# A quantised feed-forward block, from a loop of two passes to two written-out halves woven into its neighbours

## The chip, the cores and the metric

The kernel runs on one core of one Trainium2 chip. The metric is the device time of one execution in microseconds, lower is better. A core has five engines with queues of their own, which meet only through semaphores: TensorE (PE; its weight loads are PEld), VectorE (DVE), ScalarE (ACT), GpSimd (POOL) and SyncE (SP), which here issues the DMAs.

## The reference, cut to what matters

A four-layer network with 4 x 256 tokens of 256 features and a context of 4 x 256 x 64. Each layer adds a gated attention and a gated feed-forward to `x`. The change touches the end of layer 1 and all of layer 2:

```python
# layer 1, feed-forward (causal attention inside; h, mod as the code names them)
gate_pre = h @ W_in_base.T + mod * (h @ A) @ B
mlp_out  = silu(gate_pre) * (h @ W_up_base.T) @ W_down.T
x = x + tanh(g_ffn[1]) * (residual + mlp_out)
# layer 2, attention: a sigmoid of two dot products with the context, mixed with the normed rows
xij = sigmoid(si[:, :, None] + sj[:, None, :] + b)
x = x + tanh(g_xattn[2]) * (0.6 * xij + 0.4 * layernorm(x))
# layer 2, feed-forward: 256 -> 1024 -> 256, both with quantised rows and ternary weights
def bitlinear158(x, w, b): return act_quant(rms_norm(x)) @ weight_quant(w).T + b
h = gelu(silu(bitlinear158(layernorm(x), w1, b1)))
x = x + tanh(g_ffn[2]) * bitlinear158(layer_norm(h, ln_g, ln_b), w2, b2)
# act_quant: scale = 127 / max|x| of the row; round(x * scale) clipped to [-128, 127]
```

Layer 3 is an attention (`l3x`, stream C below) and a soft mixture of experts.

## The kernel before

The 1024 tokens lie in `xs`, eight tiles of 128 rows by 256 columns; a half is four tiles (two batches, `T0 = 4`). The stages run one after the other: layer 0 with its experts (to about 430 us), weights turned, stream A of `attention` (the cross attention `l1x` and the causal attention `l1f` of layer 1), the feed-forward of layer 1 with the norms of the slot vectors of layer 3 woven in, a loop of two passes over the quantised layer 2, stream C (`l3x`) and the soft experts.

**Attention.** A stream is cut into groups of eight heads, and each engine walks slices `sl` with steps `k` from 0 to 7. In slice sl TensorE computes the scores by key of group sl (`by_key`), the scores by query of group sl + 2 (`by_query`, from which VectorE takes maxima), and turns the queries and keys of group sl + 3. The slices start at sl = -3, so three slices are a prologue without an exp. Stream C has eight groups, two for each batch. For the causal attention a mask is added by a multiply with the identity: L966 writes 512 columns of a bank for the second query tile (32 times in all, for k from 2 to 5 of eight groups), L1007 512 columns for the first key tile (32 times). Both masks are zero in half of these columns. ACT's `norm` makes the normed rows of a batch once `ln_x` says that the statistics are there; for stream C `all_stats` takes them over all eight tiles.

**Feed-forward of layer 1.** `gate_and_up(h, f)` for 2 halves x 8 slices of 128 hidden columns (TensorE), a silu (L1573, ScalarE), a product (L2067 in `hidden`, VectorE); then four `down(h, i)` a half (L1210) and the additions in `add_down` (L2073). In between stand `slot_products` (L1220), `turn_slot_parts`, `spread_slots` (L1235) and, on VectorE, `slot_norms` and `scale_slots` (L2091). A gate may start once the product two before it has freed its banks.

**The quantised block.** All engines meet at a barrier (`end_of_batch`: each arrives, GpSimd clears the stage's semaphores, L445, and lets all go on), ahead of the loop and behind each of its passes. A pass takes one half: the context is copied and turned (L1262), `sj` (L1265), sigmoids (L1587); on VectorE `si`, statistics (L1667 to L1671, a root in 11 small steps), the sums L2125 to L2129, statistics again, L2135, and `quantise`; turned rows (L1273), up products (L1282), VectorE's L2158, silu (L1594), gelu (L1597), statistics of the hidden rows (L2168), gain and bias (L1678, L2175), squares (L1601), `quantise` again with the maximum L2139 and the passes L2150, L2152 and L2153; turned hidden rows (L1290 and the copy q2T), down products (L1295), and the addition L2188. TensorE fills two waits with `keep_clock`: 50 and 40 multiplies of L589 that nobody reads. GpSimd does nothing in the loop. SyncE issues the late loads for layer 3 once the feed-forward's downs are done, then arrives at the first barrier.

The order on each engine is written by hand, and each queue is strictly in that order. Eight PSUM banks are given out by hand too: gates use 0 to 3, downs 4 and 5, the slot norms 6 and 7.

Of the kernel before, what the change touches and what calls it, by code (L numbers as in the profile page):

```python
# [88 lines left out]
def maxima_landed(stream, s):  # L89
# [14 lines left out]
     "slot_sums_ps", "slot_sums", "gathered_ps", "gathered", "soft_out"),  # L104
    ("cT_ps", "sj_ps", "si", "l2x_sig", "l2x_done", "l2f_q1", "q1T_ps", "q1T", "l2f_pre", "l2f_up", "l2f_silu",
     "l2f_gelu", "l2f_stats", "l2f_ln", "l2f_sq", "l2f_q2", "q2T_ps", "q2T", "l2f_down"))
# [22 lines left out]
def flamingo(nc, I, out):  # L129
    with ExitStack() as ctx:  # L130
        sems, batch_sems = {}, []

        def once(name):

            if name not in sems:
                sems[name] = ctx.enter_context(nc.semaphore(name))
            return sems[name]
# [74 lines left out]
        quad = sb("quad", [P, 4, 32])  # L212
        region = top[0]
# [80 lines left out]
        after_operands = top[0]  # L294
        kTx = sb("kTx", [P, 2, 8, N], BF16)
# [22 lines left out]
        hT = sb("hT", [P, DC, TOKENS])  # L318
        at_f = sb("at_f", [P, B, NT, D])
        keep = top[0] - 2 * 8192  # L320


        top[0] = after_late
        gu = sb("gu", [P, HALVES, F1 // P, 512])
        sgf = [sb(f"sgf{k}", [P, 512]) for k in range(2)]
        mu2 = sb("mu2", [P, DC, SLOTS])
        atT = sb("atT", [P, DC, TOKENS])
        modT = sb("modT", [R, TOKENS])
        mh = sb("mh", [R, TOKENS])
        assert top[0] <= keep  # L330


        top[0] = after_late
        h2 = sb("h2", [P, T0, F1])
        q2 = sb("q2", [P, T0, F1], BF16)
        q2T = sb("q2T", [P, F1 // P, T0 * P], BF16)
        q1 = sb("q1", [P, T0, D], BF16)
        q1T = sb("q1T", [P, DC, T0 * P], BF16)
        xn2 = sb("xn2", [P, T0, D])
        tmp2 = sb("tmp2", [P, T0, D])  # L340
        bn2 = sb("bn2", [P, T0, 2, 6])
        c2 = sb("c2", [P, T0, CD])
        cT2 = sb("cT2", [CD, T0 * P])
# [18 lines left out]
        rcc = sb("rcc", [P, 16])  # L362

# [45 lines left out]
        assert high[0] <= nc.sbuf_usable_end  # L409

# [43 lines left out]
        def _(sp):  # L454
# [92 lines left out]
            for n in rowsF:  # L547
                W(rowsF[n][:, :], I[n].partition_broadcast(P)).then_inc(once("late_rows"), 16)
            sp.wait_ge(S("ffn_down"), T0 * HALVES)
# [7 lines left out]
            end_of_batch(sp)  # L557
            sp.wait_ge(once("batch_cleared"), B // 2 + 1 + B // 2)
# [19 lines left out]
        def _(pe):  # L578
# [304 lines left out]
            def attention(stream):  # L883
# [56 lines left out]
                def by_query(s, k):  # L940
# [16 lines left out]
                    if L == "l1f":  # L957
# [7 lines left out]
                        else:  # L965
                            mm(to[:, :], identb[:, :], mask_q[:, 1:2, :].broadcast_to([P, 2, N]), start=True, stop=False,  # L966
                               skip_group_check=True)
# [25 lines left out]
                def by_key(s, k):  # L993
# [3 lines left out]
                    to = bank[3 + n % 2]  # L997
                    if k == 0:
# [5 lines left out]
                    if L == "l1f":  # L1004
                        ti = 0 if k < 4 else 1
                        if ti == 0:
                            mm(to[:, :], identb[:, :], mask_t[:, 0:1, :].broadcast_to([P, 2, N]), start=True, stop=False,  # L1007
                               skip_group_check=True)
# [103 lines left out]
                for sl in range(-3, S_ + (1 if stream == "A" else 2)):  # L1112
                    for k in range(8):
# [58 lines left out]
            pe.wait_ge(S("at_done"), 2 * B)  # L1172
            for h in range(HALVES):
# [8 lines left out]
            for h in range(HALVES):  # L1182
# [3 lines left out]
                last.then_inc(S("mod_ps"), 1)  # L1186

# [49 lines left out]

            for f in range(F1 // P):
                gate_and_up(0, f)
            for f in range(F1 // P):  # L1240
# [3 lines left out]
                if f == 1:  # L1244
                    slot_products()
# [1239 lines left out]
```

## Time and profile before

| | us |
|---|---|
| three timed runs, median (lowest to highest) | 1382.35 (1380.15 to 1384.04) |
| the profiled execution, its own time | 1384.49 |
| its span in the trace | 1382.7 |
| PE, PEld, DVE, ACT, POOL busy | 1111.1, 689.8, 756.2, 513.8, 323.4 |
| chain that ended last: PE, DVE, ACT, issue | 69%, 20%, 4%, 4% |

Read the busy shares by stretch, not over the whole: the chain that ended last is TensorE's for two thirds, but there is a stretch of 160 us in which it is VectorE's. In a row of the timeline stand the start, the duration, engine, line, operation, what is written from what is read, the count, and in brackets how long the engine was idle before it and what released it. Rows of TensorE overlap: the pitch between starts counts, not the duration.

### The profile page before, as it was taken

What the parts mean: (1) busy time and instruction counts of PE and PEld (TensorE: products, weight loads), DVE (VectorE), ACT (ScalarE), POOL (GpSimd) and SP (SyncE); (2) the same over time, 40 slices, a digit from 0 to 9 for tenths busy, and PEclk for the clock granted to TensorE, in tenths of its full rate; (3) what the DMA queues carried; (4) which work ended last, traced back from release to release, by engine and by line L of the source; (5) the groups of instructions that cost most, each with busy time, mean ns of one, the idle gap of its engine ahead of it and who ended that gap; (6) DMA issues with size and microseconds to landing.
All of it is one profiled execution on the core that took longest, in us unless ns stands there. A gap on an engine that the chain in (4) does not pass through costs nothing.

```text
span 1382.7 us, 19444 instructions
## 1 busy us (share of the span) xinstructions
PE 1111.1 (80%) x6805; PEld 689.8 (50%) x6805; DVE 756.2 (55%) x1716; ACT 513.8 (37%) x857; POOL 323.4 (23%) x624
## 2 busy tenths in 40 slices
PE   3247999999997687887989999952535887899997
PEld 2125888888886432333555436621313443465565
DVE  4553445445444567766465111258777766577544
ACT  1112333333333565644445310014232554445443
POOL 4004344333434455324233200000001520000000
PEclk9557999999999668987999998976777899999999
DMA  6000111111301200000000200010000000000000
GB/s 152 0 0 24 46 46 46 46 46 46 106 23 59 71 2 3 2 2 2 3 2 3 107 0 0 0 46 1 0 0 0 3 2 2 0 1 9 8 1 16
DMA packets 62440, 32.05 MB, mean 23 GB/s; under 512 B 47104, under 2 KB 61072, under 8 KB 62112
## 3 DMA queue, kind: packets, MB, share of 16 engines
q1 hardware_dynamic: 62368, 31.10, 8.5%
q8 instruction: 44, 0.72, 0.2%
q14 instruction: 28, 0.23, 0.1%
HBM read 29.64 MB, written 1.05 MB: 22 GB/s over the span
## 4 chain that ended last, share of the span: by engine, by line
PE 69%; DVE 20%; ACT 4%; issue 4%; POOL 1%; SPq 1%; DMA 0%; POOLq 0%; DVEq 0%; ACTq 0%
PE bank L655 15%; PE bank L671 7%; PE bank L763 4%; PE bank L1045 3%; DVE mx L1945 3%; PE bank L1195 2%; PE bank L979 2%; PE bank L878 2%; PE bank L846 2%; PE bank L1210 2%; PE bank L1197 2%; PE bank L808 2%; PE bank L589 2%; PE bank L1025 2%; PE bank L1078 2%
## 5 line engine op out<-in xcount | busy, mean ns | idle before, releaser
L1945 DVE TENSOR_REDUCE mx<-bank 128x2 f32<-128x512 f32 (+1 forms) x176 | 118.1, 689 | 94.3 <-PE bank L979 45.2
L1503 ACT ACTIVATE prob<-bank 128x512 f32<-128x512 f32 x176 | 102.7, 597 | 105.4 <-PE bank L1025 78.8
L1342 ACT ACTIVATE hhi<-hh 128x512 fp32r<-128x512 f32 x72 | 45.5, 632 | 153.1 <-DVE hh L1782 140.5
L1778 DVE TENSOR_TENSOR hu<-bank,sg 128x512 f32<-128x512 f32 x64 | 44.2, 691 | 101.4 <-PE bank L655 101.4
L589 PE MATMUL bank<-mask_q,identb 128*128 128x512 bf16 x180 | 48.5, 439 | 62.5 <-DVE h L2175 49.1
L655 PE MATMUL bank<-xh,wh 128*128 128x512 f32 x288 | 91.5, 399 | 0.7 <-POOL wl L2293 0.7
L655 PE MATMUL bank<-xh,wl 128*128 128x512 f32 x288 | 90.6, 395 | 0.0
L655 PE MATMUL bank<-xlo,wh 128*128 128x512 f32 x288 | 90.2, 394 | 0.0
L1770 DVE TENSOR_TENSOR hlo<-hh,hhi 128x512 fp32r<-128x512 f32 x72 | 57.2, 794 | 50.8 <-ACT hhi L1342 50.8
L2293 POOL TENSOR_TENSOR wl<-wraw,wh 128x512 fp32r<-128x512 f32 x72 | 80.5, 1118 | 13.0 <-POOL wh L2290 13.0
L1381 ACT ACTIVATE sg<-bank 128x512 f32<-128x512 f32 x72 | 43.0, 598 | 65.0 <-PE bank L655 64.9
L589 PEld LDWEIGHTS bank<-mask_q,identb 128*128 128x128 bf16 x180 | 19.5, 110 | 93.7 <-DVE h L2175 50.1
L655 PEld LDWEIGHTS bank<-xh,wh 128*128 128x128 f32 x288 | 54.4, 189 | 14.5 <-POOL wl L2293 1.6
L655 PEld LDWEIGHTS bank<-xlo,wh 128*128 128x128 f32 x288 | 54.4, 189 | 13.4
L655 PEld LDWEIGHTS bank<-xh,wl 128*128 128x128 f32 x288 | 54.4, 189 | 12.4
L763 PE MATMUL bank<-mun,xT 128*128 128x512 f32 x128 | 58.1, 597 | 1.2 <-ACT xw L1342 1.2
L671 PE MATMUL bank<-hhi,wh 128*128 128x512 f32 x144 | 56.8, 394 | 0.9 <-DVE hlo L1770 0.9
L671 PE MATMUL bank<-hhi,wl 128*128 128x512 f32 x144 | 56.9, 395 | 0.0
L671 PE MATMUL bank<-hlo,wh 128*128 128x512 f32 x144 | 56.1, 390 | 0.0
L979 PE MATMUL bank<-kTx,qT 48*128 48x256 bf16 x256 | 52.5, 314 | 3.7 <-DVE kTx L1909 3.1
L1025 PE MATMUL bank<-qT,kTx 51*128 51x512 bf16 x128 | 52.9, 429 | 2.2 <-ACT prob L1503 2.1
L1945 DVE TENSOR_REDUCE mxc<-bank 128x2 f32<-128x512 f32 x64 | 42.6, 686 | 17.0 <-PE bank L979 16.0
(445 smaller groups left out, 2367.2 us busy)
## 6 DMA issues: line engine op xcount, KB each, us to landing
wraw<-in_L_ffn_wg_dram SPq DMA_DIRECT2D x64, 64.0 KB, 2.3
wraw<-in_L_ffn_wu_dram SPq DMA_DIRECT2D x64, 64.0 KB, 2.4
wraw<-in_L_ffn_wd_dram SPq DMA_DIRECT2D x32, 128.0 KB, 2.5
l_raw<-in_L_ffn_w_dram SPq DMA_DIRECT2D x2, 1024.0 KB, 7.0
mun<-in_L_ffn_mu_dram SPq DMA_DIRECT2D x1, 2048.0 KB, 7.9
xs<-in_x_dram SPq DMA_DIRECT2D x1, 1024.0 KB, 5.8
w1s<-in_L_ffn_W_dram SPq DMA_DIRECT2D x2, 512.0 KB, 7.9
stage<-in_L_ffn_W_in_base_dram SPq DMA_DIRECT2D x1, 1024.0 KB, 8.1
```

The lines of the kernel that those rows point to most:

```text
L589: mm(bank[k][:, :], identb[:, :], mask_q[:, :, :], start=True, stop=True, skip_group_check=True)
L655: last = mm(bank[4 + (n + m) % 4][:, :], w[k % 2][:, m, cc * P:(cc + 1) * P], v[:, cc, tok], start=j == 0 and cc == 0, stop=j == 2 and cc ...
L671: last = mm(bank[2 * m + h][:, :], w[k % 2][:, 2, m * P:(m + 1) * P], v[h][:, :], start=False, stop=last_pair and j == 2, skip_group_check ...
L763: last = mm(bank[n % 2][:, :], xT3[b % 2][:, cc, i * P:(i + 1) * P], mun[:, cc, ch * 512:(ch + 1) * 512], start=cc == 0, stop=cc == 1)
L979: last = mm(to[:, f * N:(f + 1) * N], t.qT[rows, s % 4, u, i * P:(i + 1) * P], key_operand(L, b, s, 8 * g + 2 * j + f, rows, slice(0, N)), ...
L1025: last = mm(to[:, :], key_operand(L, b, s, 8 * g + 2 * j, rows, slice(ti * P, (ti + 1) * P)), t.qT[rows, s % 4, u:u + 2, :], start=True, s ...
L1342: return act.activation(dst, src, ACT.Copy, scale=scale)
L1503: act.activation(t.prob[k][:, :], bank[3 + n % 2][:, :], ACT.Exp).then_inc(S("probs"), 1)
L1770: tt(hlo[k % 2][:, :], hh[k % 2][:, :], hhi[k % 2][:, :].bitcast(F32), ALU.subtract)\
L1778: tt(hu[k % 2][:, :], bank[4 + (n + 1) % 4][:, :], sg[k % 2][:, :], ALU.mult).then_inc(once("up_used"), 1)
L1945: V.reduce_max(out_, bank[n % 3][:, :].rearrange("p (h t) -> p h t", h=heads), AX, negate=True)\
L2293: G.tensor_tensor(low[:, cols, :], wraw[k][:, cols, :], high[:, cols, :].bitcast(F32), ALU.subtract)\
```

## The change

- **Masks.** L966 and L1007 write only the 256 columns of the diagonal blocks; the other half of the bank is written by the product that follows, since the first multiply opened the bank.
- **Barrier.** The loop `with Fori(0, B // 2)` and its two barriers go, and the one ahead of it moves to the end of stream A, ahead of the feed-forward. Stage semaphores count through to the end.
- **Layer 2's sigmoids** for both halves are made ahead of the gates: contexts are turned into banks 6 and 7, copied, multiplied with `l2wj` into banks 4 and 5, and ScalarE writes `sig[0]` and `sig[1]`.
- **The block in two halves.** Half 0 is written between the gates of the second half of the feed-forward; its end, with the first steps of half 1, follows the last downs. The rest of half 1 is written into stream C's prologue: turned inputs, up products and silu at (sl, k) = (-3, 7), gelu at (-2, 6), everything from the statistics of the hidden rows to the last addition at (-1, 7). Statistics for stream C are taken for each half by itself, and the `norm` of batches 2 and 3 waits for the second.
- **Feed-forward.** The slot work moves into half 0; the four downs of half 0 follow the first gate of half 1 in a row; those of half 1 use banks 0 and 1 and wait for all products.
- **Engines.** Norm, centring, rounding's second step and the scaling of the hidden rows become ScalarE activations with a bias from `l2v`; the gain and the `b2` row become GpSimd products; VectorE keeps statistics, sums, maxima and the first step of rounding. The clip is gone (the rounded value can't leave the range).
- **keep_clock** goes from the block.

```diff
@@ TensorE, by_query and by_key of the causal attention
-    mm(to[:, :], identb[:, :], mask_q[:, 1:2, :].broadcast_to([P, 2, N]), start=True, ...)
+    mm(to[:, :].rearrange("p (f n) -> p f n", f=2)[:, :, P:N], identb[:, :],
+       mask_q[:, 1:2, P:N].broadcast_to([P, 2, P]), start=True, ...)
-    mm(to[:, :], identb[:, :], mask_t[:, 0:1, :].broadcast_to([P, 2, N]), start=True, ...)
+    mm(to[:, :].rearrange("p (f n) -> p f n", f=2)[:, :, 0:P], identb[:, :],
+       mask_t[:, 0:1, 0:P].broadcast_to([P, 2, P]), start=True, ...)
@@ TensorE, by_key
+    if stream == "C" and n == 0:
+        pe.wait_ge(S("l2_rows"), 2 * T0)
@@ TensorE, stream C's slices
+    if (sl, k) == (-3, 7):
+        turn_inputs(1)
+        for i in range(T0):
+            l2_up(1, i)
+    if (sl, k) == (-1, 7):
+        l2_last(1)
@@ TensorE, ahead of and in the feed-forward
     attention("A")
     pe.wait_ge(S("at_done"), 2 * B)
+    end_of_batch(pe)
+    pe.wait_ge(once("batch_cleared"), B // 2 + 1)
...
+    for h in range(HALVES):
+        pe.wait_ge(S("modT"), h + 1)
+        for i in range(T0):
+            last = pe.transpose(bank[6 + h][0:CD, i * P:(i + 1) * P], ctxs[:, T0 * h + i, :], ident[:, :])
+        last.then_inc(S("c_turned"), 1)
+    for h in range(HALVES):
+        pe.wait_ge(S("cT2"), h + 1)
+        pe.wait_ge(S("mh"), h + 1)
+        mm(bank[4 + h][:, :], l2wj[:, :], cT8[:, h * 512:(h + 1) * 512], ...).then_inc(S("sj_ps"), 1)
...
+    # down: n == 0 waits for l2_sig, n == T0 for all 16 ffn_gu; banks (4, 0)[h] + n % 2
+    # L2_BANKS = ((4, 5, 6), (3, 4, 5)); use n of a half has bank n % 3 of these, and waits for the reader of n - 3
+def l2_last(h):
+    turn_hidden(h, 0); turn_hidden(h, 1); l2_down(h, 0); turn_hidden(h, 2)
+    l2_down(h, 1); turn_hidden(h, 3); l2_down(h, 2); l2_down(h, 3)
+for f in range(F1 // P):
+    gate_and_up(0, f)      # f == 1: slot_products, 3: turn_slot_parts, 5: spread 0 and 1, 6 and 7: spread 2, 3
+gate_and_up(1, 0)
+for i in range(T0):
+    down(0, i)
+for f in range(1, F1 // P):
+    gate_and_up(1, f)      # f == 4: turn_inputs(0), 5: l2_up(0, 0), (0, 1), 6: l2_up(0, 2), (0, 3)
 for i in range(T0):
     down(1, i)
...
-with pe.Fori(0, B // 2) as b:
...
-    keep_clock(3, 50)
...
-    keep_clock(0, 40)
...
+l2_last(0)
+pe.wait_ge(S("ffn_out"), 2 * T0)
 attention("C")
@@ ScalarE, behind the gates of half 0
+gate_silu(1, 0); gate_silu(1, 1); l2_normed(0); gate_silu(1, 2); l2_centred(0); gate_silu(1, 3)
+l2_first_quantised(0); gate_silu(1, 4); l2_inputs_turned(0); gate_silu(1, 5); l2_silu(0, 0); l2_silu(0, 1)
+gate_silu(1, 6); l2_silu(0, 2); l2_silu(0, 3); gate_silu(1, 7); l2_gelu(0, i); l2_z(0, i)      # i: all four
+l2_normed(1); l2_square(0, i); l2_second_quantised(0, i); l2_centred(1); l2_hidden_turned(0, i)
@@ ScalarE, stream C: (-3, 7): l2_inputs_turned(1), l2_silu(1, i); (-2, 6): l2_gelu(1, i)
+    if (sl, k) == (-1, 7):
+        # for all i each: l2_z, l2_square, l2_second_quantised, l2_hidden_turned
@@ VectorE, behind the products of half 0
+hidden(1, 0); scale_slots(3); add_down(0, i)                                  # i: all four
+l2_norm(0); hidden(1, 1); l2_mean(0); hidden(1, 2); l2_round_inputs(0); hidden(1, 3); hidden(1, 4)
+l2_pre(0, 0); l2_pre(0, 1); hidden(1, 5); l2_pre(0, 2); l2_pre(0, 3); hidden(1, 6); hidden(1, 7)
+l2_stats(0, 0); l2_stats(0, 1); add_down(1, 0); l2_stats(0, 2); l2_stats(0, 3); add_down(1, 1)
+l2_norm2(0); add_down(1, 2); add_down(1, 3); l2_norm(1); l2_shift(0); l2_round_hidden(0)
+l2_mean(1); l2_add(0); stats_of(step, 0.25, range(T0)); dve.sem_inc(S("ln_x"), 1); l2_round_inputs(1)
@@ VectorE, stream C: (-3, 7): l2_pre(1, i)
+    if (sl, k) == (-1, 7):
+        # l2_stats(1, i), then:
+        l2_norm2(1); l2_shift(1); l2_round_hidden(1); l2_add(1)
+        stats_of(step, 0.25, range(T0, 2 * T0))
+        dve.sem_inc(S("ln_x"), 1)
@@ VectorE, the new steps whose length matters
+def l2_shift(h):
+    for i in tiles:
+        dve.wait_ge(S("l2_zg"), T0 * h + i + 1)
+        tt(h2[:, i, :], h2[:, i, :], rowsF["L2_ffn_ln_b"][:, :], ALU.add).then_inc(S("l2_ln"), 1)
+    dve.wait_ge(S("l2_ln"), T0 * (h + 1))
+    step(V.tensor_reduce(l2v[:, 44:48], h2[:, :, :], AX, ALU.max, apply_absolute_value=True))
@@ GpSimd
+def l2_bias(h):          # rows + b2, four tiles in one product, once l2_xc is there
+def l2_gain(h):
+    for i in range(T0):
+        pool.wait_ge(S("l2_z"), T0 * h + i + 1)
+        G.tensor_tensor(h2[:, i, :], h2[:, i, :], rowsF["L2_ffn_ln_g"][:, :], ALU.mult).then_inc(S("l2_zg"), 1)
+l2_bias(0); l2_gain(0)   # then the clearing of b2s; in stream C l2_bias(1) at sl = -3, l2_gain(1) at sl = -1
@@ ScalarE, stream C's norm: one slice later (k == 0, sl + 4), batch 2 waits for ln_x 2
```

## Rows read from the trace of the kernel before

**Rows 1.** Busy time by stretch: window, length, busy (instructions) of each engine, clock, DMA.

```profile
core 0: us, PE busy (x) PEld busy (x) DVE busy (x) ACT busy (x) POOL busy (x), PEclk, DMA share, GB/s
655.00:772.70 117.70, 104.61 (x1418) 61.38 (x1416) 58.87 (x129) 58.50 (x100) 31.71 (x74) 0.96 0.03 10
...
783.20:901.70 118.50, 116.32 (x370) 63.51 (x369) 23.38 (x48) 11.58 (x19) 1.01 (x3) 0.96 0.00 0
901.70:983.70 82.00, 39.54 (x184) 19.15 (x184) 61.03 (x158) 25.54 (x31) 0.00 (x0) 0.71 0.08 20
983.70:1062.30 78.60, 39.28 (x184) 18.54 (x184) 60.94 (x158) 25.54 (x31) 0.00 (x0) 0.72 0.00 0
```

**Rows 2.** Timeline of the feed-forward, TensorE: gates, slot products, downs.

```profile
787.89 1.98 PE L1195 MATMUL bank<-hT,winT 128*128 128x512 f32 x4
...
792.58 1.98 PE L1195 MATMUL bank<-hT,winT 128*128 128x512 f32 x4
...
833.59 9.93 PE L1220 MATMUL bank<-ones,mu 128*128 128x1 f32 x64
...
850.28 1.98 PE L1195 MATMUL bank<-hT,winT 128*128 128x512 f32 x4
...
894.05 7.17 PE L1210 MATMUL bank<-wdT,gu 128*128 128x256 f32 x32 [1.71 <-DVE xs L2073]
```

**Rows 3.** Timeline at two of the barriers (902 and 984).

```profile
905.81 1.28 ACT L1342 ACT_TABLE_LOAD   x1 [24.40 <-POOLq L445]
...
983.22 0.48 DVE L2188 SCALAR_TENSOR_TENSOR xs<-bank,st,xs 128x256 f32 x1 [0.39 <-PE bank L1295]
985.06 1.28 ACT L1342 ACT_TABLE_LOAD   x1 [5.84 <-POOLq L445]
```

**Rows 4.** Groups by line and shape in the second pass: busy us, mean ns | idle before.

```profile
L2158 DVE SCALAR_TENSOR_TENSOR h<-bank,st,row_L_ffn_b 128x512 f32<-128x512 f32 x8 | 5.6, 746 | 5.2 <-PE bank L1282 4.7 <-DVE h L2158 0.2
L1295 PE MATMUL bank<-w2qT,q2T 128*128 128x256 bf16 x32 | 5.1, 334 | 0.0
L2175 DVE SCALAR_TENSOR_TENSOR h<-h,rs,row_L_ffn_ln_b 128x1024 f32<-128x1024 f32 x4 | 4.9, 1282 | 0.0
...
L2168 DVE BATCH_NORM_STATS2 bn<-h 128x6 f32<-128x512 f32 x8 | 4.8, 676 | 1.8 <-ACT h L1597 1.8
L2139 DVE TENSOR_REDUCE st<-h 128x4 f32<-128x4096 f32 x1 | 4.4, 4420 | 0.0
...
L1597 ACT ACTIVATE h<-h 128x1024 f32<-128x1024 f32 x4 | 3.9, 1045 | 0.0
...
L1667 DVE BATCH_NORM_STATS2 bn<-xs 128x6 f32 x8 | 2.8, 413 | 0.4 <-DVE st L2120 0.3
...
L1654 DVE TENSOR_TENSOR nw<-rs,ve 128x4 f32<-128x4 f32 x12 | 2.0, 163 | 0.4
```

**Rows 5.** Groups by line and shape of GpSimd over the whole span: its two-input products.

```profile
L2444 POOL TENSOR_TENSOR mu<-mun 128x4096 f32<-128x4096 f32 x1 | 7.0, 7013 | 16.7 <-DMA mun<-in_L_ffn_mu_dram 16.7
...
L2330 POOL TENSOR_TENSOR left<-qkf,qst 128x256 f32<-128x256 f32 x8 | 5.4, 670 | 0.6
...
L2412 POOL TENSOR_TENSOR qr<-xnf,row_L_ffn_ln_w 128x512 f32<-128x512 f32 x4 | 5.1, 1268 | 0.7 <-POOL tmp L2412 0.7
```

**Rows 6.** Timeline of stream C's prologue: norm of two batches, first query copy, point P.

```profile
1070.56 2.07 ACT L1479 ACTIVATE xnc<-xs,nmx,rsx 128x256 f32<-128x256 f32 x4 [12.62 <-DVEq L2195]
...
1077.42 0.69 DVE L1909 COPY qTc<-bank 96x1024 bf16<-96x1024 bf16 x1 [0.62 <-PE bank L918]
...
1090.27 2.04 DVE L1945 TENSOR_REDUCE mxc<-bank 128x2 f32<-128x512 f32 x3
```

**Rows 7.** Timeline in the causal attention, TensorE: a mask multiply and what follows.

```profile
742.46 0.39 PE L966 MATMUL bank<-mask_q,identb 128*128 128x512 bf16 x1
...
742.68 0.38 PE L970 MATMUL bank<-kTf,qT 96*128 96x256 bf16 x2
...
742.90 0.38 PE L1007 MATMUL bank<-mask_t,identb 128*128 128x512 bf16 x1
```

**Rows 8.** Instructions of one line: duration ns as min/median/max.

```profile
L1195 PE MATMUL bank<-hT,winT x64: 592/592/1201, 783.2 to 877.4; 128*128 128x512 f32 x64
```

More of the change, by code:

```diff
@@ L133, in once @@
         def once(name):
+            if name in STAGES[2]:
+                return S(name)
             if name not in sems:
@@ L1523, in attention @@
                             norm(groups[sl + 5][1])
-                        if stream == "C" and k == 5 and inside(sl + 5) and groups[sl + 5][1] >= 2 and groups[sl + 5][2] == 0:
-                            norm(groups[sl + 5][1])
+                        if stream == "C" and k == 0 and inside(sl + 4) and groups[sl + 4][1] >= 2 and groups[sl + 4][2] == 0:
+                            if groups[sl + 4][1] == 2:
+                                act.wait_ge(S("ln_x"), 2)
+                            norm(groups[sl + 4][1])
                         if k == 2 and inside(sl - 1):
@@ L2093, in _, with l2_add @@
+            def l2_add(h):
+                dve.wait_ge(S("l2_bias"), h + 1)
+                for i in tiles:
+                    row = l2_rows_of(h, i)
+                    dve.wait_ge(S("l2_down"), T0 * h + i + 1)
+                    stt(out=row, in0=of_l2(h, DOWN_USE[i])[0][:, 0:D], scalar=l2v[:, 48 + i:49 + i], in1=row,
+                        op0=ALU.mult, op1=ALU.add).then_inc(S("l2_rows"), 1)
+                dve.wait_ge(S("l2_rows"), T0 * (h + 1))
             for f in range(F1 // P):
@@ L2193, in _ @@
-            step = Steps(dve, S("dve_step"))
-            all_stats(step, 0.25)
+                if f == 4:
+                    l2_scores(0)
+                    l2_scores(1)
+                if f >= 5:
+                    scale_slots(f - 5)
+            dve.wait_ge(once("late_rows"), len(rowsF) * 16)
+            hidden(1, 0)
+            scale_slots(3)
+            for i in tiles:
+                add_down(0, i)
+            l2_norm(0)
+            hidden(1, 1)
+            l2_mean(0)
+            hidden(1, 2)
@@ new lines, in _ @@
+            l2_round_inputs(0)
+            hidden(1, 3)
+            hidden(1, 4)
+            l2_pre(0, 0)
+            l2_pre(0, 1)
+            hidden(1, 5)
+            l2_pre(0, 2)
+            l2_pre(0, 3)
+            hidden(1, 6)
+            hidden(1, 7)
+            l2_stats(0, 0)
+            l2_stats(0, 1)
+            add_down(1, 0)
+            l2_stats(0, 2)
+            l2_stats(0, 3)
+            add_down(1, 1)
+            l2_norm2(0)
+            add_down(1, 2)
+            add_down(1, 3)
```

546 lines of the change are left out of this document (343 added, 203 removed).

## Prediction

> **What bounds the kernel now.** I read, in this order, busy time by stretch, the timeline of each stretch, the groups by line of the second pass of the quantised loop, and what its ends waited for. The stretches [rows 1] show two regimes. The causal attention (655 to 773) is a TensorE stage, 104.6 of 117.7 us busy; the feed-forward (783 to 902) is one more strongly, 116.3 of 118.5, with VectorE busy for 23.4, ScalarE for 11.6 and GpSimd for 1.0. The two passes of the quantised block (902 to 984 to 1062) are the reverse: VectorE 61 of 79 to 82 us, GpSimd nothing, and TensorE's 39 us are mostly keep-clock multiplies that compute nothing. Each pass is one dependence chain on VectorE with short hops to the others, and they run one after the other. Then comes the prologue of the second attention stream, to 1090, in which the engines wait in turn. So 189 us in which no engine is full stand behind 119 us in which only one is. The change moves work from the first into the second.
>
> **Frame.** Durations are from one execution: span 1382.7 us, timed at 1384.49, which is 2.1 above the median of the three timed runs, 1382.35. I subtract from 1384.5 and then take 2 off. All is measured to one point P, at which VectorE starts the maxima of slice sl = 0 of stream C, 1090.27 [rows 6]; behind it the change alters only the place of two norms.
>
> **Diagonal masks.** 32 mask multiplies of L966 and 32 of L1007 go from 512 to 256 columns. A 512-column one takes a pitch of 0.22 us, and the two 256-column ones behind it share 0.22 [rows 7]. 64 x 0.11 = 7.0 us of TensorE. The stage is 89% TensorE [rows 1]; the rest of it waits for copies and maxima that don't shrink, so 3 to 7 arrive; I take 5.
>
> **The head of the feed-forward.** The barrier now stands ahead of it. Its price is the way from VectorE's last result of a pass (983.70) to ScalarE's start, 985.06, less a hop: 1.3 us [rows 3]. New on TensorE ahead of the first gate: two sets of four f32 context transposes, the first beside the second tanh, then a wait for ScalarE's copy of the second set (0.6 us and two hops of 0.2), then two 512-column f32 products of two passes each. A pass of 512 columns has a pitch of 0.43 to 0.5 (four in 1.98 [rows 2]), so 0.5 for the set, 1.0 for the copy, 1.8 for the products: 3.3 to 3.5. The gates start at 783.2 + 1.3 + 3.5 = 788.0. The eight sigmoids (0.5 each by [rows 6], and a table load of 1.3 [rows 3]) are covered by the first gate.
>
> **Half 0 of the feed-forward.** A gate-and-up takes 4.68 us (787.89 to 792.58), the slot products 9.9, the gate behind them 6.8 because the clock had fallen, two downs 7.2 less 0.4 of overlap [rows 2]. Nine gates 42.1, slot products 10, slow gate 2.2, four downs 13.5, spreading the slots with a wait for their norms 3.2: T = 859.0, the end of the four downs. Merely a new order, no cost.
>
> **Half 0 of the quantised block, beside gates 1 to 7.** Prices [rows 4]: a root 2.2 us (11 steps of 0.2), statistics of four rows 1.4, of four hidden rows 4.8, a 1024-column pass of VectorE over two tensors 1.2, one of a hidden half from PSUM 0.75, ScalarE 0.5 for 256 columns [rows 6] and 1.0 for 1024. Relative to T:
> First norm (statistics 1.4, sum 1.2, aggregate, root, scales) done at 6.6. ScalarE's norm to 8.7. Mean sent at 12.3, but its root holds VectorE to 14.5, so hidden(1, 2) is late and TensorE waits 1.1 us. Inputs rounded at 18.6, quantised 19.2, turned 20.6. Up products wait for their three banks: 1.9 us on TensorE, twice. The last gate ends at 38.5. The downs of half 1 now use banks 0 and 1 and wait for hidden(1, 7), 1.4 us; they end at 53.2. So the feed-forward ends at 912, not 901.7: it pays 10 us.
> Behind it VectorE is the chain again: norm of half 1 to 59.7, shift to 64.6, the 4.4 us maximum to 69.0, root and scales to 72.4, rounding to 75.4, mean of half 1 to 81.1. ScalarE's centring of half 1 stands ahead of the turned hidden copies, so these start at 81; copies, turns and downs alternate over three banks, the last row is added at 88.1, statistics of its four tiles end at 92.5. ln_x comes at 951.5, against 1070.5 now.
>
> **GpSimd's gain.** The gain multiply leaves VectorE for GpSimd. No row has 1024 columns of two f32 inputs there. 256 columns take 0.67, 512 take 1.26, 4096 of one tensor with itself 7.0 [rows 5]. Bounds: 1.75 (a quarter of the last), 2.45 (the slope of the first two). It has two tensors, as those two have, so 2.45; four are 9.8 us. In half 0 they hide behind the last downs and the norm of half 1. In half 1 nothing hides them. While they run, VectorE shifts the rows before, an operation with two SBUF inputs. No row shows such a pair side by side: 0 to 1.2 us for each of three overlaps; I take 3 us in all.
> The Trainium skill (GPSIMD Engine Reference, Key points) says that GpSimd shares its SBUF interfaces with VectorE and contends with VectorE instructions that have two SBUF inputs. By that rule the upper end holds, 1 us above my sum; no row of before shows it.
>
> **The prologue, with the front of half 1 in it.** From the norm (1070.56) to P took 19.7 us [rows 6]. Now, relative to T: norm at 92.6, half 1's inputs rounded on VectorE at 95.9, queries and keys by 101, then in sl = -3 the turned inputs, eight up products and eight VectorE passes of 0.75, to 109.4. The slices sl = -2 and -1 take VectorE 12.3 more, as before (1077.42, less its copy, to 1090.27): 121.7. ScalarE's silu, gelu and two table loads (10.8 us) fit beside.
>
> **The tail of half 1, at (sl, k) = (-1, 7).** It stands in every queue ahead of sl = 0: VectorE's maxima, TensorE's by_key(0, 0) and ScalarE's first exp are behind it. It is serial: statistics 4.9, root 3.2, first z 1.2, gains 9.8 + 3, last shift 1.3, maximum 4.45, root and scales 3.45, first rounding 0.8, four quantised rows 4.0 on ScalarE (all ahead of the first turned copy), the alternation of copies, turns, downs and adds 8.7 (four copies of 1.0 and four downs of 1.3 [rows 4], less their overlap), statistics of four tiles 4.6. Sum 49.4, less 2.8 where rounding and quantising overlap: 46.6. P' = 859.0 + 121.7 + 46.6 = 1027.3. So 63.0 us are gained to P, though some 47 of a pass of 79 stay in the open.
>
> **Removed.** Two barriers of 1.3 and one of 4.1, at 902, which waited for SyncE to issue its late loads [rows 3]: these are inside the 63, as are the keep-clock multiplies. VectorE didn't wait for those (TensorE waited for it), so they give nothing, and without them turns and downs run at the lower clock, counted above. SyncE now issues the late loads beside the block.
>
> **Sum.** 1384.5 - 63 - 5 = 1316.5 on the profiled basis, 1314.5 on the median's: 1315.
>
> **Rivals.**
> (a) The tail is longer. GpSimd slowed to the full (1 to 4 us), 0.2 us at some 30 hand-overs not in my sum (6), gates waiting for VectorE at six more places, 1 us each (6). For it: in a pass of today VectorE is idle for 18 of 79 us [rows 1]. 1325 to 1332. Chance 0.24.
> (b) The tail is shorter: gains at 1.75 without contention (6 us), masks worth all of 7. 1302 to 1308. Chance 0.18.
> (c) The change does what its name promises, all of half 1 beside the prologue: another 40 us, 1275. Against it, all three queues have the tail ahead of sl = 0. Chance 0.02.
> (d) Slower than before, by the clock. If gates stall on VectorE, TensorE's granted clock falls from 2.4 to 1.2 GHz, as for the gate from 843 to 850, where a multiply took 1.20 instead of 0.59 [rows 8]. Seven gates and eight downs at the lower level cost 33 + 27 = 60 us; with (a) on top it is 1385 to 1392. It decides from the point at which nearly every gate stalls; I count waits of 1.1 and 1.4 us in 54, and TensorE is busy for 116.3 of 118.5 today. Chance 0.03.
> (e) The masks give nothing because the maxima's path binds: 1320, inside the forecast.
> The forecast itself, 1308 to 1325: 0.53.
>
> **Range and chances.** 1301 to 1336 leaves out (c), (d) and the outer ends of (a) and (b), together 0.2 at most. 0.3% (4 us) is about what a measurement of this kernel can tell from no change. Faster 0.97, same 0.01, slower 0.02 (the upper part of (d)).
>
> **What will show it.** On the new trace: the first gate near 783 (788 less the masks), four downs in a row that end near 854, the last L1-down near 907; gains of 1.8 to 3.5 us each on GpSimd; VectorE idle ahead of the shifts of half 1 but hardly ahead of those of half 0; the first exp of stream C at 1016 to 1022; TensorE's clock at its upper level through the feed-forward, below it in the tail. The core is wrong if the tail isn't 40 to 55 us long, or if the stretch from the first gate to the last L1-down grew by more than 12 us from 118.5.

## The result, and the profile after

| | us |
|---|---|
| changed kernel, four timed runs, median (lowest to highest) | 1329.76 (1327.55 to 1335.26) |
| kernel before, beside it | 1382.86 (1380.15 to 1384.04) |
| ratio, 95% interval | 0.9625 (0.9592 to 0.9657) |
| profiled execution of the changed kernel, its own time; span | 1327.55; 1325.7 |

The change gains 53 us (57 between the two profiled spans, 1382.7 and 1325.7). 1315 was forecast, with a range of 1301 to 1336: the time lies in the range, 15 above the forecast, where rival (a) was put.

The changed kernel by stretch, to be held against [rows 1]: causal attention, feed-forward from the first gate to the last down, from there to `ln_x`, the prologue of stream C with the front of half 1, the tail of half 1. Columns: window, length, busy (instructions) of each engine, granted clock, DMA.

```profile
core 0: us, PE busy (x) PEld busy (x) DVE busy (x) ACT busy (x) POOL busy (x), PEclk, DMA share, GB/s
650.00:761.10 111.10, 96.77 (x1416) 60.85 (x1414) 58.87 (x129) 57.66 (x100) 31.72 (x74) 0.97 0.03 10
776.50:905.80 129.30, 123.82 (x393) 68.01 (x393) 51.58 (x137) 33.79 (x52) 4.32 (x2) 0.92 0.00 1
905.80:953.00 47.20, 8.69 (x64) 6.57 (x64) 38.77 (x98) 17.48 (x26) 16.76 (x14) 0.63 0.14 34
953.00:982.70 29.70, 18.39 (x249) 10.20 (x250) 23.34 (x40) 18.70 (x23) 13.52 (x26) 0.73 0.01 2
982.70:1031.50 48.80, 10.83 (x75) 7.52 (x75) 34.41 (x80) 19.36 (x23) 13.86 (x8) 0.57 0.00 0
```

The feed-forward is 10.8 us longer than in [rows 1] and now carries a third of VectorE's work from the first gate to P (51.6 of 148.1 us). Two stretches stay in which VectorE is the chain and TensorE mostly stands, 47 and 49 us, where before there were two passes of about 80. The clock there is 0.57 to 0.63.

The account between the two profiles: to the first causal scores 5.0 less (650.5 to 645.5; nothing was changed ahead of that, and a second profile of the changed kernel has its first causal scores 3.7 later again, so most of this is a difference between executions); from there to the first gate 1.7 less; from the first gate to P 255.0 instead of 307.1, 52.1 less; behind P 1.8 more. The forecast for gate to P was 239.3, so 15.7 us of the gain didn't come. The miss lies here. Against the 68 us forecast between the two profiles, 57 came: 15.7 less here and 1.8 less behind P, 1.5 more ahead of the gate, and 5.0 more at the start, which is no gain of the change.

Timeline of half 0's block beside the gates: start, duration, engine and line, operation, operands, count, idle time before. The first three rows are the last steps of a root.

```profile
861.69 0.16 DVE L1838 TENSOR_TENSOR nw<-rs,ve 128x4 f32<-128x4 f32 x1
861.88 0.16 DVE L1839 SCALAR_TENSOR_TENSOR nw<-nw,rs 128x4 f32<-128x4 f32 x1
862.08 2.19 DVE L1840 SCALAR_TENSOR_TENSOR rs<-nw,rs 128x4 f32<-128x4 f32 x1
864.31 0.69 DVE L2275 TENSOR_TENSOR gu<-bank,sgf 128x512 f32<-128x512 f32 x1
865.05 3.78 PE L1253 MATMUL bank<-hT,winT 128*128 128x512 f32 x4 [3.16 <-DVE gu L2275]
```

An operation on four numbers a row takes 2.19 us instead of 0.16. The product behind it comes 2 us late, TensorE waits 3.16 instead of the 1.1 forecast, and its next gate runs at the lower clock (3.78 for four multiplies, 1.98 in [rows 2]; the granted clock from 865 to 871 is 0.59). What stood beside it is on GpSimd's timeline:

```profile
861.89 2.36 POOL L2712 TENSOR_TENSOR xs<-xs,row_L_ffn_b 128x1024 f32<-128x1024 f32 x1 [89.69 <-ACT xn L1711]
903.85 10.25 POOL L2721 TENSOR_TENSOR h<-h,row_L_ffn_ln_g 128x1024 f32<-128x1024 f32 x4 [39.59 <-ACT h L1738]
915.24 3.51 POOL L2730 MEMSET kTc<- 3x4096 bf16 x1
```

The first is the b2 row, two inputs in SBUF, from 861.89 to 864.25: it ends where the held step ends. The other two stand beside the norm of half 1. VectorE there:

```profile
905.80 0.48 DVE L2281 SCALAR_TENSOR_TENSOR xs<-bank,gates,xs 128x256 f32<-128x256 f32 x1 [2.79 <-PE bank L1270]
906.32 1.41 DVE L2312 BATCH_NORM_STATS2 bn<-xs 128x6 f32<-128x256 f32 x4
907.64 1.96 DVE L2313 TENSOR_TENSOR sig<-sig,xs 128x1024 f32<-128x1024 f32 x1
909.63 0.38 DVE L2314 BATCH_NORM_AGGREGATE mv<-bn 128x2 f32<-128x6 f32 x4
910.05 1.78 DVE L2315 TENSOR_SCALAR ve<-mv 128x4 f32<-128x4 f32 x1
911.86 2.55 DVE L1831 TENSOR_SCALAR nw<-ve 128x4 int32<-128x4 int32 x1
914.45 0.17 DVE L1832 TENSOR_SCALAR rs<-nw 128x4 int32<-128x4 int32 x1
914.65 0.16 DVE L1838 TENSOR_TENSOR nw<-rs,ve 128x4 f32<-128x4 f32 x1
...
916.42 2.35 DVE L2319 TENSOR_SCALAR l2v<-rs,gates 128x4 f32<-128x4 f32 x1
```

Read them by kind. With a bank and one SBUF input (L2281), as statistics (L2312) or as aggregate (L2314) VectorE isn't disturbed by the gain (0.48, 0.35 a tile, 0.38). Two SBUF inputs (L2313: 1.96 for 1.21) and a scalar operation from SBUF to SBUF (L2315, L1831: 1.78 and 2.55 for 0.17) are. Beside the clearing of `kTc`, from 915.24 to 918.75, which reads nothing, two-input steps such as L1838 still took 0.16, but the scalar one, L2319, was held until 918.77. The four held operations cost 6.9 us together. Reductions go on as well: the maximum L2382 takes 4.42 both times, in the tail with two small products of GpSimd beside its start, and in the trace of before the 176 reductions of `mx` (L1945) take 0.69 each, 78 of them beside GpSimd.

The tail of half 1, VectorE and GpSimd, at the gain and the shift:

```profile
L2721 POOL TENSOR_TENSOR h<-h,row_L_ffn_ln_g x4: 2350/2840/3333, 992.0 to 999.9; 128x1024 f32<-128x1024 f32 x4
L2380 DVE TENSOR_TENSOR h<-h,row_L_ffn_ln_b x4: 1214/3359/3365, 994.4 to 1004.3; 128x1024 f32<-128x1024 f32 x4
```

(Instructions of the tile by line, duration in ns as min/median/max.) The first two gains take 2.35 and the last shift, alone, 1.21; the last two gains and the first three shifts take 3.3 each, which is nearly the one and the other added (2.35 and 1.15).

### The profile page after: what moved, and what is told of

Same layout as the page of the kernel before. It is cut to its first block, busy times and chain, and to the rows that moved or that the text cites. A ratio compares the mean times of both kernels' runs of the same rounds, so it can differ in the third digit from the quotient of the medians.

```text
span 1325.7 us, 19063 instructions
## 1 busy us (share of the span) xinstructions
PE 1054.8 (80%) x6622; PEld 672.0 (51%) x6625; DVE 741.9 (56%) x1676; ACT 534.6 (40%) x891; POOL 354.0 (27%) x634
## 4 chain that ended last, share of the span: by engine, by line
PE 67%; DVE 21%; ACT 4%; issue 4%; POOL 2%; DMA 0%; SPq 0%; POOLq 0%; DVEq 0%; ACTq 0%; PEldq 0%
PE bank L692 15%; PE bank L708 7%; PE bank L800 4%; DVE mx L2130 3%; PE bank L1084 3%; PE bank L915 2%; PE bank L883 2%; PE bank L1270 2%; PE bank L845 2%; PE bank L1253 2%; PE bank L1016 2%; PE bank L1064 2%; PE bank L1255 2%; PE bank L1117 1%; DVE h L2380 1%
## 5 line engine op out<-in xcount | busy, mean ns | idle before, releaser
L1963 DVE TENSOR_TENSOR hu<-bank,sg 128x512 f32<-128x512 f32 x64 | 44.2, 691 | 102.1 <-PE bank L692 102.1
L692 PEld LDWEIGHTS bank<-xlo,wh 128*128 128x128 f32 x288 | 54.6, 190 | 13.5
L1337 PE MATMUL bank<-identb,q 128*128 128x128 bf16 x64 | 7.5, 289 | 62.9 <-ACT q L1750 62.9
L1064 PE MATMUL bank<-qT,kTx 51*128 51x512 bf16 x128 | 52.1, 424 | 2.5 <-ACT prob L1594 2.5
L2543 POOL CAST wh<-wraw 128x512 fp32r<-128x512 f32 x72 | 37.6, 522 | 59.4 <-PE bank L692 30.7
```

The lines of the kernel that those rows point to most:

```text
L692: last = mm(bank[4 + (n + m) % 4][:, :], w[k % 2][:, m, cc * P:(cc + 1) * P], v[:, cc, tok], start=j == 0 and cc == 0, stop=j == 2 and cc ...
L1064: last = mm(to[:, :], key_operand(L, b, s, 8 * g + 2 * j, rows, slice(ti * P, (ti + 1) * P)), t.qT[rows, s % 4, u:u + 2, :], start=True, s ...
L1963: tt(hu[k % 2][:, :], bank[4 + (n + 1) % 4][:, :], sg[k % 2][:, :], ALU.mult).then_inc(once("up_used"), 1)
```

## Experiments

All are timed against the kernel before on the same chip. Two measures are given: the ratio, whose interval is 2 to 4 us each way, and from each trace the time from the start of the fourth addition of half 0 (850 or so; 0.2 behind T, which is read here as the start of the gate behind the four downs, 847.88 in the changed kernel) to four marks. These agree between executions to 0.1 us: 57.7 to the last addition of half 1's downs, 99.9 to the last row of the block's half 0, 178.3 to that of half 1, 179.2 to the first exp of stream C, in both profiles of the changed kernel. What differs is what lies outside: the first gate lay between 776.5 and 782.8, from the first causal scores to it passed 129.5 to 131.5 in the changed kernel and its variants, and from the first exp to the end 297.0 to 300.9.

**The changed kernel again**, as a measure.

> The changed kernel as it is, beside the other two on one chip, as their measure. Theory and rival alike: 1330 to 1332, a ratio to the kernel before of 0.9625 with an interval of 0.003 each way. In its trace the stretches from the first gate on are as long as in the first trace to 0.3 us, and the starts of the stages ahead of it may lie some us apart.

1330.5 us, ratio 0.9618 (0.9593 to 0.9642). Marks 57.7, 99.95, 178.3, 179.25. First gate at 780.2, not 776.5.

**Masks alone**, on the kernel before: the two mask edits of the diff.

> The kernel before, with the two mask multiplies cut to the diagonal blocks and nothing else changed. Theory (TensorE's pitch): 64 multiplies shrink by 0.11 us, and in the trace of the changed kernel the stretch from the first to the last mask multiply is 96.4 us long where it was 102.0; so 5.6 us less, 1377 from 1382.6. Rival 1 (the whole 7.0 us of TensorE's time arrive and the stage behind gains too): 1375 or less. Rival 2 (the path runs over VectorE's maxima, and the shorter stretch came from another part of the change): within 2 us of the kernel before.

1376.0 us, ratio 0.9932 (0.9910 to 0.9955), 9 us with 3 each way. The trace is sharper: in both kernels the first causal score comes at 650.4 to 650.5, the gates at 783.21 before and here at

```profile
776.12 1.98 PE L1195 MATMUL bank<-hT,winT 128*128 128x512 f32 x4
```

7.1 us earlier. That is rival 1's amount, all of TensorE's 64 x 0.11. The estimate of 5.6 went by the stretch between the first and the last mask of one line, which leaves out a part of the stage.

**Gain on VectorE**, both halves.

```diff
# GpSimd (the line of half 1 goes with its condition on the slice)
-l2_gain(0)
-l2_gain(1)
# VectorE, in l2_shift, ahead of the shifts
+for i in tiles:
+    dve.wait_ge(S("l2_z"), T0 * h + i + 1)
+    tt(h2[:, i, :], h2[:, i, :], rowsF["L2_ffn_ln_g"][:, :], ALU.mult).then_inc(S("l2_zg"), 1)
```

> The changed kernel, with the gain product of both halves on VectorE in front of the shift; GpSimd keeps the b2 row only. Theory (one engine waits for the other's whole operation when VectorE has two inputs in SBUF or a scalar operation over one): in the changed kernel the first z to the last shift of half 1 takes 14.8 us; here one z and eight passes of 1.23 give 11.1, so 3.7 less. In half 0 the norm of half 1 loses its waits (4.9 us in four operations beside the gain), pays 4.9 for the gain, and keeps about 2 for GpSimd's clearing: 0 in sum. In all 1326. Rival (no exclusion: GpSimd's product merely has a length of 2.7 us, and VectorE's norm is late for another reason): half 0 pays 4.9, half 1 gains 3.7, 1331, and the norm of half 1 still shows operations of about 2 us in the same places.

1325.0 us, ratio 0.9556 (0.9535 to 0.9578). Marks 57.7, 99.0, 174.0, 175.0: half 0 0.9 less, half 1 3.4 less. L2313 is back at 1.21 and L1831 at 0.17; L2315, now beside the clearing of `kTc`, is the one that is held. So taking work from VectorE made its path longer: with the gain back (4.6 us a half) each half is shorter, by 0.9 and by 3.4.

**b2 row later**: half 0's behind `keys(0)` of stream C, half 1's behind `l2_gain(1)`.

> The changed kernel, with GpSimd's addition of the b2 row moved: half 0's behind the gain and the first keys of stream C, half 1's behind the gain of half 1. Theory (the addition held VectorE's root step for 2.0 us, so TensorE stood for 3.2 us and the gate behind ran at the lower clock level): the step at that place takes 0.16 instead of 2.19, TensorE waits 1.1 us as forecast, the gate loses its 2.4 us: the feed-forward's last down ends 4.4 us earlier, and the time is 1325.4. Rival (the long step has another cause, or the clock falls at a wait of 1.1 too): the last down ends at most 2 us earlier, 1328 to 1330.

1330.8 us, ratio 0.9604 (0.9581 to 0.9628). Marks 55.0, 96.9, 178.5, 179.5.

```profile
863.66 0.16 DVE L1840 SCALAR_TENSOR_TENSOR rs<-nw,rs 128x4 f32<-128x4 f32 x1
863.86 0.69 DVE L2275 TENSOR_TENSOR gu<-bank,sgf 128x512 f32<-128x512 f32 x1
864.47 1.21 DVE L2347 TENSOR_REDUCE l2v<-xn 128x4 f32<-128x1024 f32 x1
864.60 3.68 PE L1253 MATMUL bank<-hT,winT 128*128 128x512 f32 x4 [1.13 <-DVE gu L2275]
```

The step is 0.16 long, TensorE's wait is the forecast 1.13, and the downs end 2.75 earlier, not 4.4: the gate is at the lower level behind a wait of 1.13 too (granted clock 0.52 from 864.6 to 868.1). In half 1 the gain is given back, for the b2 row now stands beside the last shift, and holds it (the four shifts take 13.21 instead of 11.07):

```profile
994.26 13.21 DVE L2380 TENSOR_TENSOR h<-h,row_L_ffn_ln_b 128x1024 f32<-128x1024 f32 x4 [3.80 <-POOL h L2722]
...
1003.07 3.32 POOL L2713 TENSOR_TENSOR xs<-xs,row_L_ffn_b 128x1024 f32<-128x1024 f32 x1
...
1007.50 4.42 DVE L2382 TENSOR_REDUCE l2v<-h 128x4 f32<-128x4096 f32 x1
```

The theory of the hold stands twice. Of the 2.4 us that I put on the clock only 0.7 came, and the whole time shows no gain over the changed kernel.

**Copies interleaved**, on ScalarE.

```diff
-for i in range(T0): l2_second_quantised(0, i)
-l2_centred(1)
-for i in range(T0): l2_hidden_turned(0, i)
+# q: l2_second_quantised, t: l2_hidden_turned
+q(0, 0); q(0, 1); t(0, 0); q(0, 2); t(0, 1); q(0, 3); t(0, 2); t(0, 3); l2_centred(1)    # half 1 the same
```

> The changed kernel, with another order on ScalarE alone: the copies of the turned hidden rows stand between the second quantised rows (two, then one and one), and in half 0 ahead of the centring of half 1. Theory (ScalarE's order puts 1.6 us of centring with its wait of 1.3, and two quantised rows, ahead of the first copy, and VectorE's additions wait for it): the last row of half 0 comes 4 us earlier, that of half 1 2 us earlier, 1324. Rival (VectorE's root of the second mean, which ends at 940.7, or the alternation of three banks sets these times): 0 to 1.5 us, 1328 to 1330.

1325.6 us, ratio 0.9576 (0.9558 to 0.9594). Marks 57.7, 96.05, 172.15, 173.1: 3.9 in half 0 and 2.2 in half 1, as forecast.

**The three together** (b2 row of half 1 where the changed kernel has it).

> The changed kernel with three edits at once: the gain of both halves on VectorE, ScalarE's copies between the quantised rows, and GpSimd's b2 row of half 0 behind the first keys of stream C (that of half 1 where the changed kernel has it). Theory (the three waits lie on different stretches of one chain): 4.3 for the gain, 6.1 for the order of the copies, 2.8 for the b2 row of half 0, as the traces of the single edits show them: 13 less than the changed kernel, 1317, a ratio to the kernel before of 0.952. Rival (they shorten the same waits, since all three lie ahead of VectorE's additions): 8 less, 1322.

1317.6 us, ratio 0.9541 (0.9517 to 0.9565). Marks 54.9, 93.8, 166.0, 167.0: 12.3 us less, the sum of the parts (4.3 + 6.1 + 2.8) to 0.9. They lie on different stretches of one chain.

**Root behind the product**, on top of these: `hidden(1, 2)` between the sending of the mean and its root.

> The three edits together, and VectorE's root of the second statistics of half 0 behind the product of gate 2 instead of ahead of it. Theory (TensorE's remaining wait of 1.1 us ahead of a gate in the second half of the feed-forward comes from that root, and the gate behind it runs at the lower clock level, 1.8 us longer): the wait goes, the last down ends 2.9 us earlier; the rounding of the inputs comes 0.7 later but has room. 1314, ratio 0.950. Rival (the clock falls at the next small wait, or the up products are late by the 0.7): 0 to 1 us.

1316.4 us, ratio 0.9526 (0.9496 to 0.9556). Marks 54.45, 93.3, 165.75, 166.7: only 0.3 to 0.5 less. The wait of 1.1 is gone (one of 0.64, for the quantised inputs, stands in its place), and the last gate ends at T + 37.4 (39.6 without this edit, 42.4 in the changed kernel; the forecast was 38.5). But the clock takes it back in the downs. Without this edit, and with it:

```profile
890.55 14.08 PE L1270 MATMUL bank<-wdT,gu 128*128 128x256 f32 x64 [1.41 <-DVE gu L2280]
```

and

```profile
889.04 15.77 PE L1270 MATMUL bank<-wdT,gu 128*128 128x256 f32 x64 [1.41 <-DVE gu L2280]
```

The same 1.41 us of waiting for the last product is followed by downs of 14.08 in one (granted clock 1.00) and 15.77 in the other (0.89). The statistics kernel below, which has this edit too, repeats it: 15.77 and 0.89. This is the fastest kernel of the study, though not measurably faster than the one without its last edit.

**Without the tail.** The end of half 1 is left out.

> The changed kernel without the end of half 1: hidden statistics, norm, gain, shift, maximum, rounding, turns, downs and additions of half 1 are left out, the statistics for stream C stay. What is left out took 48.8 us from 982.66 to 1031.49, of which the 4.6 of the statistics for stream C stay. Theory (the end of half 1 is wholly in the open, since it stands in all three queues ahead of slice 0 of stream C): 44 us less, 1286. Rival (part of it lies beside work of stream C, which then shows in its place): 35 less or fewer, 1295 or more.

1285.8 us, ratio 0.9307 (0.9280 to 0.9334), 44 us below the changed kernel. First exp at 132.9 instead of 179.2, 46.3 earlier, while VectorE takes the last maxima of the prologue; P comes 44.2 earlier, which is the 48.8 of the tail less the 4.6 that stay. All of the tail is in the open; the theory stands.

**Clock kept in the tail**: ahead of `l2_last(1)`, `pe.wait_ge(S("l2_ln"), 2 * T0)` and `keep_clock(5, 30)`.

> The changed kernel with 30 multiplies of 512 columns that nobody reads on TensorE during the maximum of half 1's hidden rows, into a bank that is free then. Theory (the turns and downs of half 1 and the first multiplies of slice 0 run at the lower clock level: 1.7 to 1.9 us for eight multiplies where it is 1.04 at the upper): turns and downs 1 to 2 us shorter, 1328. Rival 1 (ScalarE's copies of 1.0 set the pace of this stretch): no change, 1330. Rival 2 (the multiplies run into the turns): up to 2 us more, 1332.

1334.3 us, ratio 0.9654 (0.9629 to 0.9678); first exp at 178.8, 0.4 earlier. The turns ahead of the first two copies took 0.62 for eight, but ScalarE's quantised rows and those copies, 1.02 each in both kernels, set the pace there.

```profile
1022.85 1.90 ACT L1435 ACTIVATE q2T<-bank 128x1024 bf16<-128x1024 bf16 x2
1025.91 1.02 ACT L1435 ACTIVATE q2T<-bank 128x1024 bf16<-128x1024 bf16 x1 [1.16 <-PE bank L1339]
1028.41 1.02 ACT L1435 ACTIVATE q2T<-bank 128x1024 bf16<-128x1024 bf16 x1 [1.47 <-PE bank L1339]
```

The outcome is that of rival 1, no gain, but only the front of the stretch was tested: the extra multiplies end at 1018.9, the granted clock is 1.00 from there to 1024.8 and 0.64 from 1024.8 to 1029.5, where the second downs take 1.91 and ScalarE waits for TensorE's turns (1.16 and 1.47 above). What a clock kept up to the last downs would give isn't shown. The kernel's median is even 4 us above that of the changed kernel, with intervals that touch; its first gate came at 782.8, ahead of everything that was edited, from the fourth addition to the first exp it isn't longer, and from there to the end it took 300.9, against 298.3 in both profiles of the changed kernel. I don't count this as an effect.

**Statistics of half 1 later**, on top of the root's kernel: `stats_of` at (0, 3), the norm of batch 2 at (0, 4).

> The kernel with the root behind the product of gate 2, and besides: the statistics of half 1 for stream C stand behind VectorE's maxima (0, 3) instead of ahead of slice 0, and ScalarE's norm of batch 2 at (0, 4) instead of (0, 0). Theory (in the changed kernel ScalarE waits 3.4 us for these statistics behind its first exp, and TensorE 4.1 us for the next one): that wait goes, and the 4.6 us of statistics lie in a slice where VectorE has room; 3 less, 1313, a ratio to the kernel before of 0.950. Rival (GpSimd's splitting of the queries of batch 2 comes late and slice 1 waits for it, or VectorE has no room in slice 0): the wait comes back a slice later, within 1 us of the kernel without this edit.

1321.1 us, ratio 0.9551 (0.9525 to 0.9576); against 0.9526 no gain. The wait moved four exps on, and TensorE's with it (4.58), and from the first exp to the end 299.1 passed instead of 297.1:

```profile
1018.77 0.60 ACT L1594 ACTIVATE probc<-bank 128x512 f32<-128x512 f32 x1 [0.16 <-PE bank L1064]
1019.87 0.60 ACT L1594 ACTIVATE probc<-bank 128x512 f32<-128x512 f32 x1 [0.25 <-PE bank L1064]
1024.75 1.09 ACT L1570 ACTIVATE xnc<-xs,nmx,rsx 128x256 f32<-128x256 f32 x2 [4.28 <-DVEq L2249]
```

Rival: VectorE has no room for 4.6 us in slice 0 either.

**Shift behind all gains**: the wait for `l2_zg` ahead of each shift is for all four. It is written for both halves; in half 0 the gains end 5 us ahead of the first shift as it is.

> The changed kernel, with VectorE's shifts of half 1 waiting for all four gains of GpSimd instead of one each. Theory (a product of GpSimd and a two-input operation of VectorE never run at the same time): the gains take 2.35 each instead of 2.35 to 3.33, the shifts 1.15 each instead of 3.36, and the stretch from the first z to the start of the maximum stays within 0.6 of its 14.8 us: 1.3 + 9.4 + 4.6 = 15.3. The time stays the same. Rival (they run side by side, both slowed): without the neighbour the gains take 2.35, but the shifts, which lay beside them, are added: a stretch of at least 14.8 + 2.5, 1332.5 or more. Rival 2 (GpSimd's 2.8 us are its own length for this shape): gains of 2.8, a stretch of 17.

1334.0 us, ratio 0.9643 (0.9618 to 0.9668), against 0.9618 beside it: no difference that the intervals tell apart. The trace decides:

```profile
994.78 9.25 POOL L2721 TENSOR_TENSOR h<-h,row_L_ffn_ln_g 128x1024 f32<-128x1024 f32 x4 [13.57 <-ACT h L1738]
...
1004.06 4.67 DVE L2380 TENSOR_TENSOR h<-h,row_L_ffn_ln_b 128x1024 f32<-128x1024 f32 x4 [10.70 <-POOL h L2721]
1008.76 4.42 DVE L2382 TENSOR_REDUCE l2v<-h 128x4 f32<-128x4096 f32 x1
```

First z (993.46) to maximum (1008.76): 15.3, as the theory had it to the tenth, and 14.8 in the changed kernel. Taking away all overlap by order cost 0.5 us, so there was hardly any; the rival put 2.5 or more on it.

## Why the prediction was right, and where it was 15 us short

The measured time lies in the range because the sum had the right chain and most of its terms; it doesn't lie in the forecast's own band, 1308 to 1325. The 15.7 us that are missing between the first gate and P lie in half 0 of the feed-forward (0.4), in half 0's block (4.7), in the norm of half 1 (6.7), between it and the tail (1.7) and in the tail (2.2). The signs that were to show a wrong core didn't come: the tail is 48.8 long (40 to 55 was asked) and the feed-forward's stretch grew by 10.8 (12 at most); the first exp missed its sign, 1027.3 instead of 1016 to 1022.

- **Masks.** Forecast 5 of 3 to 7. Measured 7.1 alone; in the changed kernel 6.4 (132.7 to the first gate became 130.95 with a head of 4.6; three later kernels have 129.5 there). The part taken off for copies and maxima wasn't there.
- **Head.** Forecast 4.8. From the last row of stream A's result to the first gate 11.3 us before, 15.9 now: 4.6. Right. Only its parts differ: TensorE waits 2.52 for the barrier, and some products behind it run at the lower clock.
- **Half 0 of the feed-forward.** First gate to T forecast 71.0, measured 71.4.
- **Half 0's block.** Norm done at T + 6.5 (6.6 forecast), mean sent at 12.1 (12.3). Then the hold at L1840 that the sum didn't have: gates end at 42.4 instead of 38.5, downs at 57.9 instead of 53.2. 4.7 us; moving the b2 row returns 2.75 of it, and with the root moved as well the last gate ends at 37.4. That is 1.1 better than the sum, the wait of 1.1 that this edit takes away. What the sum calls two waits of 1.9 for the banks of the up products came as time and not as waits: each set of eight products holds TensorE for 1.7 to 1.9 us by its own length, which the sum had nowhere else, and it waited 0.16 for them.
- **Norm of half 1.** Ends at T + 71.1, forecast 59.7: 4.7 inherited and 6.7 of holds by the gain and the clearing. This is the step that failed: "In half 0 they hide behind the last downs and the norm of half 1", and 0 to 1.2 us for each overlap. In half 0 a moved operation was priced by its own length alone, and its neighbour's delay by nothing. What shows that was there to read in the trace of before. In the experts' stage the same two kinds stand side by side (durations in ns as min/median/max):

```profile
L1770 DVE TENSOR_TENSOR hlo<-hh,hhi x72: 691/693/1265, 127.6 to 436.7; 128x512 fp32r<-128x512 f32 x72
L2293 POOL TENSOR_TENSOR wl<-wraw,wh x72: 729/1141/1312, 119.6 to 425.3; 128x512 fp32r<-128x512 f32 x36, 128x256 fp32r<-128x256 f32 x36
```

  A VectorE subtraction of two SBUF inputs, 0.69 alone, reaches 1.27. "No row shows such a pair side by side" was wrong: the groups by line show a mean, and the maximum of a line had to be asked for. Held steps of four and eight columns stand there too, the second held by the clearing of `kTc` itself. Two pairs, each VectorE's step and GpSimd's operation beside it:

```profile
15.46 4.05 DVE L1648 TENSOR_SCALAR rs<-nw 128x4 int32<-128x4 int32 x1
11.06 8.43 POOL L2235 TENSOR_SCALAR_AFFINE_SELECT picks<-picks 128x4096 bf16<-128x4096 bf16 x2
...
1066.95 0.83 DVE L1685 TENSOR_SCALAR vex<-mvx 128x8 f32<-128x8 f32 x1
1064.24 3.51 POOL L2455 MEMSET kTc<- 3x4096 bf16 x1
```

  Both steps take 0.17 alone, and both end within 0.03 us of the end of their neighbour.
- **From there to P.** Shift, maximum, rounding and mean as forecast. Half 0's last row came at T + 100.6 (88.1), `ln_x` at 105.1 (92.5), slices -2 and -1 ended at 134.8 (121.7): hardly more than inherited.
- **Tail.** Forecast 46.6, measured 48.8; the experiment without it shows that 44 to 46 are in the open. The sum for z, gains and shifts was right (15.3 against 14.8), in part by luck: 1 us for each overlap, chosen between 0 and 1.2, is nearly what it costs when nothing overlaps, the 1.15 of a shift, and a gain takes 2.35 alone (2.45 forecast). What was too small is the end. From the first rounding to the last addition 13.6 us passed; the sum had 13.5 less 2.8 "where rounding and quantising overlap". That overlap needs the order that the copies experiment made, which gave 2.2 of it.
- **Behind P.** 1.8 us more (294.2 instead of 292.4). ScalarE's norm of batch 2 waits 3.4 us for half 1's statistics behind the first exp, and TensorE 4.1 us behind it. The prediction took nothing for the moved norm. That the wait makes the 1.8 isn't shown: placing it later only moved it, and kernels that have it in the same place took 292.8 to 296.7 behind P.
- **Removed keep-clock multiplies.** That they give nothing wasn't tested by itself. Put back in front of the turns of half 1 they give 0.4 us, as far as they keep the clock.
- **Rivals.** (a) came in its time, but not in the place that it names: only 2.2 of the 15.7 lie in the tail, and these are the order of the copies. Its first cause, GpSimd's neighbours, acted ahead of the tail and more strongly than priced; its waits at more gates are nearly absent (beside the one at 865 TensorE waited in this stretch only for the last product, 1.41 as forecast); its hand-overs weren't measured one by one. (b) came by half: the masks gave all of 7, but the gain takes 2.35 and not 1.75. (e) didn't come. (c) is 44 us further, as large as put. (d) didn't come: the granted clock of the feed-forward is 0.92 against 0.96.

The Trainium skill (SBUF — State Buffer, "Who interferes with whom") says that GpSimd and VectorE share one pair of ports, that an operation gets it for its whole length while the other is blocked, and which VectorE operations ask for it: those with two SBUF inputs, against a GpSimd operation that reads, and copies or scalar operations in a two-port mode, against any. The trace agrees in each case: L1838 free and L2319 held beside a clearing (0.16 and 2.35 us), L2313 held beside a product (1.96), L2281 and L2314 free; that the scalar operations ran in a two-port mode is not shown by itself. The prediction had weighed a shorter statement of it as 1 us above its sum (0.6 by its own bound of 1.2 for each overlap), and only in the tail. Read as exclusion, and with the measured 2.35 us of a product, it lets the b2 row hold a step for up to its own length and leaves no overlap between gains and shifts.

Open is why the clock stays up after one wait of 1.4 us and falls after another, and why the stages ahead of the change start up to 6 us apart between executions.

## What to carry to other kernels

Work moved from VectorE to GpSimd ran here in parallel only to VectorE operations that read a bank, take statistics or reduce; beside an operation with two SBUF inputs, or a scalar one from SBUF to SBUF, it was serial, and even a 0.16 us step can be held for the 2.3 us of a product. So give GpSimd short products, and place them beside VectorE's idle time or reductions, or leave them where they were. Judge a change of a few us by marks relative to one event inside the program, since these repeat to 0.1 us where whole times of one kernel differ by up to 8, but remember that they don't see what lies outside. And look at a line's maximum in the trace of before, not only at its mean.

## What the runs showed of the hardware that was not expected

- A GpSimd product of 1024 columns, 2.35 us, holds a VectorE step of four columns for up to 2.55 us. In the other direction a gain waits for a shift: 3.33 for 2.35.
- A clearing that reads nothing (3.51 us) holds scalar operations (L2319 2.35 for 0.23, and L2315 1.26 for 0.17 in the kernel with the gain on VectorE), not two-input ones (L1838 0.16).
- TensorE's clock: behind a wait of 3.16 and behind one of 1.13 a gate ran at the lower level (3.78 and 3.68 for four multiplies), behind a wait of 1.41 the downs did in part in two kernels (15.77, granted clock 0.89) and didn't in others (14.08, granted clock 1.00).
